# Message-passing kernel, second layer: weighted source rows in rounded high and low parts and one 512-column matmul per chunk, in place of a weighted one-hot matrix and a full-precision matmul

## The reference

```
all_msg = einsum('nf,rfo->rno', h, weight)
msg = all_msg[rel_type, src] * norm            # norm: one number per edge
gate = sigmoid(all_gate[rel_type, src])[:, None]
agg = segment_sum(msg * gate, dst, num_segments=n_nodes)
x = layernorm(x + relu(agg))
```

## Time and profile before

| | |
|---|---|
| median of 3 runs | 1801.48 us (1800.02 to 1804.83) |
| span of the profiled execution | 1798.2 us |
| first gather of the second layer | at 1179.3 us |
| last gather of the second layer | at 1761.5 us |
| PE busy over the span | 1322.6 us (74%) |
| POOL busy over the span | 890.4 us (50%) |
| DVE busy over the span | 921.7 us (51%) |
| ACT busy over the span | 492.7 us (27%) |

### The profile page before, as it was taken

The page is one execution under the profiler, slowest core; times in us unless marked ns, Lnnn a source line. Parts: engine busy times, 40 slices in busy tenths (PEclk is TensorE's granted clock), DMA queues, the critical chain, the costliest instruction groups (busy, mean ns, idle before and its releaser), DMA issues.

```text
span 1798.2 us, 21483 instructions
## 1 busy us (share of the span) xinstructions
PE 1322.6 (74%) x6758; PEld 1088.5 (61%) x6758; DVE 921.7 (51%) x1914; ACT 492.7 (27%) x1069; POOL 890.4 (50%) x905
## 2 busy tenths in 40 slices
PE   5799999458999999999999999943424444444444
PEld 4788888447878787878787888732313323332333
DVE  5744444468777777787878787221212222222222
ACT  3222222304454545454444444500000000000000
POOL 1041000476565656565656563057576666666661
PEclk9899999769999999999999999965556666666666
DMA  7454446566676767776767675333333333333331
GB/s 143 130 152 145 135 133 225 151 191 181 209 238 210 238 208 232 217 238 207 238 211 238 209 239 161 106 111 110 87 110 99 105 102 103 104 103 103 104 102 44
DMA packets 103851, 286.56 MB, mean 159 GB/s; under 512 B 20805, under 2 KB 40409, under 8 KB 100661
## 3 DMA queue, kind: packets, MB, share of 16 engines
q0 software_dynamic: 56032, 169.34, 31.5%
q1 hardware_dynamic: 47774, 116.71, 21.3%
HBM read 189.33 MB, written 96.65 MB: 159 GB/s over the span
## 4 chain that ended last, share of the span: by engine, by line
PE 56%; issue 24%; DVE 7%; DMA 6%; POOL 3%; ACT 1%; SPq 1%; another core or an unknown queue 1%; DVEq 0%; ACTq 0%; POOLq 0%
PE bank L954 14%; PE bank L837 11%; PE bank L865 10%; PE bank L795 5%; PE bank L729 5%; DMA kv_table<-tstage 4%; PE bank L783 2%; POOL kv L651 2%; PE bank L813 2%; PE bank L751 2%; PE bank L737 1%; DVE kv L1367 1%; PE bank L757 1%; POOL kv L637 1%; DVE S L1372 1%
## 5 line engine op out<-in xcount | busy, mean ns | idle before, releaser
L637 POOL DMA_INDIRECT kv<-kv_table,rows x416 | 458.6, 1102 | 304.9 <-PE bank L865 130.9
L651 POOL DMA_INDIRECT kv<-message_table,rows x416 | 395.7, 951 | 264.7 <-issue 123.5
L954 PE MATMUL bank<-kv,onehot_w 128*121 128x256 f32 x832 | 276.1, 463 | 336.7 <-issue 300.8
L954 PEld LDWEIGHTS bank<-kv,onehot_w 128*121 128x121 f32 x832 | 186.6, 226 | 426.2 <-issue 389.8
L837 PE MATMUL bank<-wr_r,x1T_r 128*121 128x512 f32 x1248 | 324.8, 403 | 2.2 <-ACT mstage L1098 2.2
L837 PEld LDWEIGHTS bank<-wr_r,x1T_r 128*121 128x121 f32 x1248 | 217.7, 183 | 51.9 <-ACT mstage L1098 3.3
L1504 DVE SCALAR_TENSOR_TENSOR z<-bank,xb 121x256 f32<-121x256 f32 x26 | 10.9, 420 | 429.7 <-remote 280.1
L1098 ACT ACTIVATE mstage<-bank,gate 121x256 f32<-121x256 f32 x416 | 171.0, 470 | 149.9 <-PE bank L837 137.3
L865 PE MATMUL bank<-kv,onehot_r 128*121 128x264 f32 x832 | 202.4, 392 | 0.0
L1176 ACT ACTIVATE sd<-mv,eps 121x1 f32<-121x1 f32 x26 | 7.7, 295 | 604.5 <-DVE mv L1510 513.4
L865 PEld LDWEIGHTS bank<-kv,onehot_r 128*121 128x121 f32 x832 | 150.3, 186 | 29.0
(11 more groups left out here) (135 smaller groups left out, 1397.7 us busy)
## 6 DMA issues: line engine op xcount, KB each, us to landing
message_table<-mstage SPq DMA_DIRECT2D x104, 484.0 KB
kv_table<-tstage SPq DMA_DIRECT2D x26, 1210.0 KB
kv<-kv_table,rows POOLq DMA_INDIRECT x416
kv<-message_table,rows POOLq DMA_INDIRECT x416
query_table<-qstage_r SPq DMA_DIRECT2D x26, 242.0 KB
qb_r<-query_table SPq DMA_DIRECT2D x26, 242.0 KB
kv<-in_Wr POOLq DMA_DIRECT2D x2, 2048.0 KB, 14.6
xb<-in_x SPq DMA_DIRECT2D x26, 121.0 KB
```

The lines of the kernel that those rows point to most:

```text
L637: pool.indirect_dma_start(kv[:, n % 2, u, 0:2 * C], None, ktab, bass.IndirectOffsetOnAxis(ap=rows[:, 0, n, u:u + 1], axis=0)).then_inc(kv_ ...
L651: pool.indirect_dma_start(mrows[:, r.q, u, :], None, mtab, bass.IndirectOffsetOnAxis(ap=rows[:, 1, r.number, u:u + 1], axis=0)).then_inc(l ...
L954: last = mm(b_l[r.q][:NODES, 0:C], onehot_w[:, r.q, u, :], mrows[:, r.q, u, :], start=(u == 0), stop=(u == U - 1))
```

## The change

The one-hot matrix of a round holds only ones and zeros again (`mark`, in `onehot_r`, two rounds deep, one round ahead), and the weights go to the rows. ACT multiplies each chunk's rows by `norm` and writes them rounded to `float32r` (`weigh_high`). DVE makes the rest, `mrows * norm - high`, with one `scalar_tensor_tensor` per chunk, also `float32r` (`weigh_low`). High and low part of a chunk lie side by side in `rows_r`, which is the room of the first layer's weights `wr_r`, two rounds deep. PE does one `float32r` matmul per chunk, with 512 columns. PSUM then holds two sums; ACT copies the low one to SBUF (`keep_low_sum`), DVE adds the two and goes on as before. Landings and weighing are counted in four groups of four chunks. POOL's wait before a round is for the low parts of the round four earlier, where it was for the sum.

Order of work in a round r: ACT does high group 0 of r, the low sum and the square root of r - 1, and high groups 1 to 3 of r. DVE does low group 0 of r, `finish` of r - 1, `mark` of r + 1, and low groups 1 to 3 of r.

```diff
@@ gather_messages (POOL)
-                    pool.wait_ge(l_agg, r.again)
+                    pool.wait_ge(l_low, G * r.again)
                 for u in range(U):
                     pool.indirect_dma_start(mrows[:, r.q, u, :], None, mtab,
                                             bass.IndirectOffsetOnAxis(ap=rows[:, 1, r.number, u:u + 1], axis=0)
-                                            ).then_inc(l_landed[r.q][u * 2 // U], 16)
+                                            ).then_inc(l_landed[r.q][u // GU], 16)
@@ l1 (PE)
-                    if u % (U // 2) == 0:
-                        pe.wait_ge(l_landed[r.q][u * 2 // U], r.used)
-                    last = mm(b_l[r.q][:NODES, 0:C], onehot_w[:, r.q, u, :], mrows[:, r.q, u, :],
+                    if u % GU == 0:
+                        pe.wait_ge(l_low, r.parts(u // GU))
+                    last = mm(b_l[r.q][:NODES, 0:2 * C], onehot_r[:, r.par, u, :],
+                              rows_r[:, r.par, u, :, :].rearrange("p k c -> p (k c)"),
                               start=(u == 0), stop=(u == U - 1))
@@ ACT
+            def keep_low_sum(f):
+                act.wait_ge(l_agg, f.done)
+                wait(act, l_sum, f.halves(0))
+                a(low_sum[:, :], b_l[f.q][:NODES, C:2 * C], ACT.Copy).then_inc(l_sum, 1)
+
+            def weigh_high(r, g):
+
+                if g == 0 and r.reuses:
+                    act.wait_ge(l_agg, r.two_back)
+                act.wait_ge(l_landed[r.q][g], r.used)
+                j = bass.ds(r.number, 1)
+                for u in range(g * GU, g * GU + GU):
+                    last = a(rows_r[:, r.par, u, 0, :], mrows[:, r.q, u, :], ACT.Copy, scale=norms[:, j, u])
+                last.then_inc(l_high, 1)
+
+            def l1(r):
+                weigh_high(r, 0)
+                if not r.first:
+                    keep_low_sum(r.back())
+                    out_deviation(r.back())
+                for g in range(1, G):
+                    weigh_high(r, g)
@@ finish (DVE)
-                    sums = b_l[f.q]
                     dve.wait_ge(l_agg, f.done)
+                    b = b_l[f.q]
+                    dve.wait_ge(l_sum, f.halves(1))
+                    v.tensor_tensor(z[:NODES, :], b[:NODES, 0:C], low_sum[:, :], ALU.add).then_inc(l_sum, 1)
+                    dve.wait_ge(l_sum, f.halves(2))
+                    sums = z
@@ DVE
-            def weigh_onehot(r):
...
+            def mark(r):
+
+                if r.reuses:
+                    dve.wait_ge(l_agg, r.two_back)
                 j = bass.ds(r.number, 1)
                 for u in range(U):
-                    last = v.tensor_scalar(onehot_w[:, r.q, u, :], iota_n[:, :], dstl[:, j, u], norms[:, j, u],
-                                           ALU.is_equal, ALU.mult)
+                    last = v.tensor_scalar(onehot_r[:, r.par, u, :], iota_n[:, :], dstl[:, j, u], None, ALU.is_equal)
                 last.then_inc(l_oh, 1)
+            def weigh_low(r, g):
+
+                dve.wait_ge(l_high, r.parts(g))
+                j = bass.ds(r.number, 1)
+                for u in range(g * GU, g * GU + GU):
+                    last = v.scalar_tensor_tensor(rows_r[:, r.par, u, 1, :], mrows[:, r.q, u, :], norms[:, j, u],
+                                                  rows_r[:, r.par, u, 0, :].bitcast(F32), ALU.mult, ALU.subtract)
+                last.then_inc(l_low, 1)
+
             def l1(r):
-                if not (isinstance(r.i, int) and r.number + 2 >= ROUNDS):
-                    weigh_onehot(r.ahead())
-                finish(r)
+                weigh_low(r, 0)
+                if not r.first:
+                    finish(r.back())
+                if not (isinstance(r.i, int) and r.number + 1 >= ROUNDS):
+                    mark(r.ahead())
+                for g in range(1, G):
+                    weigh_low(r, g)
```

More of the change, by code:

```diff
@@ L107, in __init__ @@
         self.again = i * LB + (q - 5)
-        self.used = i * 128 + (128 if q >= 2 else 0)
+        self.two_back = i * LB + (q - 3)
+        self.used = i * (16 * GU) + (16 * GU if q >= 2 else ROUNDS // 2 * 16 * GU)
     @property
@@ L121, in stores_before, with halves, parts, first @@
         return self.i * (16 * LB) + 16 * (self.q - 2)
+    def halves(self, k):
+        return self.i * (2 * LB) + (2 * (self.q - 2) + k)
+    def parts(self, g):
+        return self.i * (LB * G) + ((self.q - 2) * G + g + 1)
+    @property
+    def first(self):
+        return isinstance(self.i, int) and self.number == 0
+    @property
+    def reuses(self):
+        return not (isinstance(self.i, int) and self.number < 2)
     def ahead(self):
-        return Turn(self.eng, self.i, self.q + 2) if self.q < 2 else Turn(self.eng, self.i + 1, self.q - 2)
+        return Turn(self.eng, self.i, self.q + 1) if self.q < LB - 1 else Turn(self.eng, self.i + 1, 0)
+    def back(self):
+        return Turn(self.eng, self.i, self.q - 1) if self.q else Turn(self.eng, self.i - 1, LB - 1)
 def turns(eng, body):
@@ L267, in build @@
                 x1T_r = msb("x1T_r", [P, 2, 2, HALVES, NODES], F32R)
-            onehot_w = lsb("onehot_w", [P, LB, U, NODES])
+            onehot_w = lsb("onehot_w", [P, 1, U, NODES])
+            low_sum = hm[:, 0, :]
+            rows_r = wr_r[:, :, :, :, :].rearrange("p b h r c -> p b (h r) c").rearrange(
+                "p b (u k) c -> p b u k c", k=2)
             mrows = kv[:, :, :, :].rearrange("p b u c -> p (b u c)")[:, 0:LB * U * C].rearrange(
@@ L316, in build @@
         oh_ready = sem("oh_ready")
-        kv_landed = [sems(f"kv_landed{p}_", G) for p in range(2)]
+        rows_landed = [sems(f"rows_landed{q}_", G) for q in range(LB)]
+        kv_landed, l_landed = rows_landed[0:2], rows_landed
         ohT_filled, ohT_ready = sems("ohT_filled", G), sems("ohT_ready", G)
@@ L336, in build @@
         x1_stored = sem("x1_stored")
-        l_oh, l_agg = sem("l_oh"), sem("l_agg")
-        l_landed = [sems(f"l_landed{q}_", 2) for q in range(LB)]
+        l_oh, l_high, l_low, l_agg = sem("l_oh"), sem("l_high"), sem("l_low"), sem("l_agg")
         l_x = sems("l_x", 2)
@@ L342, in build @@
             "l_z", "l_st", "l_mv", "l_sd", "l_rstd", "l_y"))
-        l_out = sem("l_out")
+        l_out, l_sum = sem("l_out"), sem("l_sum")
         fill_ready, overfull_ready = sem("fill_ready"), sem("overfull_ready")
@@ L1172, in _, with out_deviation @@
                 keep_message(f, c)
-            def l1(f):
+            def out_deviation(f):
                 act.wait_ge(l_mv, f.done)
                 a(sd[:NODES, :], mv[:NODES, 1:2], ACT.Sqrt, bias=eps[:NODES, :]).then_inc(l_sd, 1)
-            rounds(act, l1)
+            def keep_low_sum(f):
[17 more added lines that the diff above has]
+                    weigh_high(r, g)
+            turns(act, l1)
+            keep_low_sum(Turn(act, QUADS, LB - 1))
+            out_deviation(Turn(act, QUADS, LB - 1))
             with general(act):
@@ L1197, in _ @@
                 tiles(act, tile0)
-                tiles(act, l1)
+                tiles(act, out_deviation)
         @block.vector
@@ L1516, in finish @@
                                 ALU.subtract, ALU.mult).then_inc(l_y, 1)
-            def weigh_onehot(r):
-                if r.refills:
-                    dve.wait_ge(l_agg, r.again)
+            def mark(r):
+                if r.reuses:
+                    dve.wait_ge(l_agg, r.two_back)
                 j = bass.ds(r.number, 1)
                 for u in range(U):
-                    last = v.tensor_scalar(onehot_w[:, r.q, u, :], iota_n[:, :], dstl[:, j, u], norms[:, j, u],
-                                           ALU.is_equal, ALU.mult)
+                    last = v.tensor_scalar(onehot_r[:, r.par, u, :], iota_n[:, :], dstl[:, j, u], None, ALU.is_equal)
                 last.then_inc(l_oh, 1)
-            def l1(r):
-                if not (isinstance(r.i, int) and r.number + 2 >= ROUNDS):
-                    weigh_onehot(r.ahead())
-                finish(r)
+            def weigh_low(r, g):
[5 more added lines that the diff above has]
+                last.then_inc(l_low, 1)
+            def l1(r):
+                weigh_low(r, 0)
[5 more added lines that the diff above has]
+                    weigh_low(r, g)
             dve.wait_ge(x1_stored, 16 * ROUNDS)
             dve.wait_ge(m_filled[1], ROUNDS * MB)
-            for q in (2, 3):
-                weigh_onehot(Turn(dve, 0, q))
+            dve.wait_ge(agg_done, ROUNDS * G)
+            mark(Turn(dve, 0, 2))
             turns(dve, l1)
+            finish(Turn(dve, QUADS, LB - 1))
             with general(dve):
```

## The result

The changed kernel takes 1858.91 us (median of 4 runs, 1854.91 to 1863.64) where the kernel before takes 1803.15 us beside it: ratio 1.0315 (1.0298 to 1.0332), slower by 56 us. The profiled execution has a span of 1854.9 us. The forecast was 1855 us.

What follows compares the result with a forecast made beforehand. It took the stage as bound by the gathers' pace and by late PE work and semaphores. Span 1798.2 + 44 (pace) + 10 (tail) + 3.3 (to the median) = 1855 us; range 1745 to 1920, forecast's own 1815 to 1900.

Steps and rivals of the forecast that it cites:

- The mechanism: Second layer: each round becomes a chain ACT, DVE, PE, DVE, with PE's late hop in it once per round.
- The forecast hop: PE's finished sum reaches waiting engines late while POOL gathers: 17.5 us or more if as in round 0.
- The order of work around the hop: Behind `finish` of r - 1, waiting for PE's sum, stand three quarters of the low parts and the next one-hot matrix.
- two of its own signs: Forecast wrong if `finish` starts within 1 us of PE's last matmul during unbroken gathers, or the tail shrinks below 30 us.
- Pauses: POOL's timeline: a pause after every 16 gathers of over 3 us would mean the forecast.
- The line 0.78 + 0.145 us per gather: POOL's pause lengths before the change: 0.78 us + 0.145 us for each gather since the last pause.
- The pace: Second layer's time per round: 24.5 us where it was 22.4, over 21 rounds, +44 us.
- The tail: From last gather to end of span, 36.7 us before: 2.3 rounds at 14 us, taken as +10 us.
- Gathers held up: A low part on DVE delays a gather by 0.35 us at most; 1 us per round, ends 0 and 5.6.
- Rival D: Gathers held up for the low parts' whole length: POOL bound at 25.7 us per round, 1866 us; chance 0.05.
- A: Pace stays 22.4 us per round, gathers served at 1.40 us, longer chain fits: 1800 to 1818 us; chance 0.19.
- B: PE's lateness goes and POOL issues without pauses: 1745 us (1720 to 1775); chance 0.25.
- C: Late hop met twice per round, or a round waits through two POOL runs: 28 us or more, 1930 us; chance 0.06.

Runs made afterwards that it cites:

- e2: The changed kernel without low parts; PE and POOL wait for the high parts instead: 1847.5 us, 1.0245.
- e10: The kernel before with 16 further DVE instructions a round of the low part's form, results unused, outside every chain: 1815.2 us, 1.0079.
- e7: The changed kernel with a round's marks in one DVE instruction of 1936 columns in place of 16 of 121: 1823.9 us, 1.0124.
- e1: The changed kernel, but low parts subtract a PSUM bank, so that the DVE instruction has one SBUF input only: 1866.4 us, 1.0346.
- e12: e1 with a POOL memset of 512 columns, 0.55 us, ahead of every four gathers: 1848.0 us, 1.0258.
- e6: The changed kernel, reordered: ACT and DVE weigh all four groups before the previous round's sum and finish: 1861.0 us, 1.0351.
- e8: The changed kernel with both edits, that of e6 (rows first) and that of e7 (one mark instruction): 1822.9 us, 1.0120.
- e9: The kernel before, but each gather fetches 128 columns (512 bytes) per row in place of 256: 1800.1 us, 1.0003.
- e4: The kernel before with 2 of 16 matmuls per round, all gathers, one-hots and waits kept: 1792.7 us, 0.9951.
- e13: e7 with a POOL memset of 512 columns, 0.55 us, ahead of every four gathers: 1821.0 us, 1.0113.

## Why the prediction was right, step by step

**The mechanism: right in its place, wrong in its engine.** The prediction had said that each round becomes a chain ACT, DVE, PE, DVE in which what is slow beside the gathers is met every round. Two pairs of runs show that the chain is needed. e2 has hardly more DVE instructions than before and half of PE's records, and loses 45 us, some 20 of them between the gathers. e10 has the DVE instructions without the chain, and loses 15 us, 9 of them after the last gather. What is slow in the chain of the changed kernel is another thing than forecast: not one late hop from PE, which is prompt in 22 of 26 rounds, but DVE's own instructions, 1.40 us apart. PE fires its four matmuls of a group together (2.06 us) and waits. The forecast hop does come, up to 35 us late, in runs with 22 and 23 DVE instructions a round (e2, e7), and not in those with 38 in the same order of work (the changed kernel, e1, e12). So the count of DVE instructions alone does not give the loss either: 22 cost 45 us (e2), 23 cost 22 (e7), 38 cost 56. The order of work around the hop, on which the prediction spent most of its words, is worth nothing (e6, e8).

By two of its own signs the forecast's mechanism is wrong, though the time is right. It named a `finish` that starts within 1 us of PE's last matmul while POOL gathers without a break, and a tail under 30 us. `finish` starts 0.5 to 0.6 us behind the matmul in 18 of 26 rounds, two of them (at 1245.0 and 1297.5 us) ahead of POOL's first pause and of any held-up gather; the tail is 22.1 us.

**Pauses.** It expected one after every 16 gathers, of over 3 us. There are three in all, of 14 to 17.5 us, since for about four rounds the ring lets DVE work at 13.4 us per round. The line 0.78 + 0.145 us per gather held for the kernel before (and e9, e10) and gives 19.3 us where 17.5 and 16.1 were measured, 5.4 where e1 has 11.5, and 49.5 where e4 has 1.68. It is not a law of the gathers alone.

**The pace.** 24.5 us per round was taken between 22.4 and 27.4; it is 25.6. The wait that was to make it, PE's late hop once per round, did not occur; DVE's slow instructions stood in its place. With the rounds before the first pause the term is +69 us where +44 was predicted.

**The tail.** +10 us was taken from 0 to +16; it is -14.6. This step failed: the estimate let some two rounds run one after the other behind the last gather. But the last pause ends at 1748.32 us, the rounds of 13.5 us that follow it catch up with POOL, and little more than the last round is left when the last row lands. This hangs on where the last pause falls: e1, whose last pause ends at 1801.37 us, has 50.0 us behind its last gather, and e12 46.5, close to the 36.7 + 10 of the estimate. The two errors, -25 and +25 us, cancel, and that is luck; the time of 1855 us is closer than its steps deserve.

**Gathers held up.** 1 us per round was taken from bounds of 0 and 5.6; it is 83.2/26 = 3.2 us. The reading of the earlier trace rows, that a gather waits for the running instruction and not for the row of them, fell: back to back, 16 low parts of 0.40 us hold one gather for all of them. The Trainium skill ("SBUF — State Buffer", section "Who interferes with whom") calls contention on the port pair that DVE and GpSimd share an exclusive lock. The gathers of 6.23 and 6.73 us agree with it. That a gather waits for a whole row of such instructions is shown by these rows alone. Rival D's mechanism still didn't come about: at most one gather a round meets such a row, and e1 shows that most of what it loses would be a pause otherwise. That D's numbers (25.7 us per round, 1866 us) lie so close to the measured ones is luck as well: e1, without any held-up gather, runs at 26.0 us per round.

**Durations.** Low parts 0.40 us back to back for 0.35, marks 0.20 to 0.21 for 0.257, high parts 6.47/16 = 0.40 for 0.42.

**Rivals.** A (22.4 us per round stays) is what e10 does, and not the change. B (no pauses, 1.254 us per gather) came about in no run: e4, with PE nearly empty, comes down to 1.40 us per gather, and PE's load was not what stood in its way. C (28 us or more per round, by a hop met twice) came in none: with a hop 25 to 35 us late in 12 of 26 rounds e2 takes 24.4 us per round.

**What stays open.** Which part of the chip serves gathers at 1.40 us and holds other engines back meanwhile is not shown by any row. Nor is what makes the same wait show as slow DVE instructions in one run and as a late semaphore in another. e12 (38 instructions, slow) and e13 (23, fast) don't settle the part of the count, since the gathers came 1.38 us apart in the one and 1.48 in the other, on either side of 1.40. Why e7, with one DVE instruction a round more than e2 and held-up gathers, is some 22 us faster than it (ratios 1.0124 and 1.0245) is open too; that its held-up gathers are the breaks that help was not tested.

## What to carry to other kernels

Look at the spacing of an engine's short instructions beside a stream of indirect DMAs: where 0.3 us of work comes every 1.4 us with nothing that it waits for, busy time no longer says what the engine can do. Look as well at how long an engine stands idle after the work that it waits for has ended. Work that frees the gathers' buffers is a bad place for a new chain through several engines: e2's chain, with no low parts, cost 45 us, and e10's 16 instructions outside it 15. Gathers that are stretched by another engine, as here, need not be the bound; take the stretch away alone and see whether it comes back as a wait. A forecast that hits by two wrong terms that cancel has to be read by its terms.

## What the runs showed of the hardware that was not expected

- Gathers of 128 rows went no faster than about 1.40 us each over the layer in any run (582.2 us for 416 in the kernel before, 580.8 with 2 of 16 matmuls), with 1 KB or 512 B per row alike, while POOL can issue one per 1.25 us for the first 170 or so. In the two kernels named the rows of each still arrive 2.3 to 3.5 us after its start, so it is not their transfer that lags.
- A sum that PE had finished was taken up by ACT up to 35.5 us later while gathers ran (e2), and within 0.1 us in most rounds of the changed kernel.
- After POOL has stopped, DVE stays slow for some time: 12 us after the stretch that ended at 1526.96 us.
- A POOL memset of 0.34 us ahead of every four gathers cost 6 us over the layer and gave back 16 us at its end.
